# A three-layer network in float32 on one core: head and expert stages rebuilt, with a new order of VectorE's work at the first experts

## The chip, the cores and the metric

The kernel runs on one core of a Trainium2 chip. The metric is the device time of one execution in microseconds (us). It is given as the median of several runs; beside it stands one profiled execution, from which every row of the trace below comes. The engines are TensorE (PE; its weight loads are PEld), VectorE (DVE), ScalarE (ACT), GpSimd (POOL) and SyncE (SP), which issues all the DMAs.

## The reference, cut to what matters

The input is x of 4 sequences x 512 tokens x 128 features, 2048 tokens in all. Four residual layers follow one another:

```python
x = x + ssm(layernorm(x))          # state-space layer with 64 complex states, a scan over the 512 tokens
x = x + experts(layernorm(x))      # 8 experts, each token weighted by its best 2
x = x + attention(layernorm(x))    # 16 heads of 64, a relative-position bias, softmax over 512 keys
x = x + experts(layernorm(x))      # the same experts and weights again

def experts(xt):                   # router_w 8x128, w_gate/w_up 8x128x256, w_down 8x256x128
    top, idx = top_k(xt @ router_w.T, 2)
    g = sigmoid(top); g = g / (g.sum(-1) + 1e-10)
    for e in range(8):
        ge = sum(where(idx == e, g, 0))
        out += ge[:, None] * ((silu(xt @ w_gate[e]) * (xt @ w_up[e])) @ w_down[e])
```

Every expert is computed for every token and multiplied by its gate, which is zero for most tokens.

## The kernel before

The 2048 tokens are four chunks of 512. A large matrix product is made of three passes over numbers that are split into a rounded high part and a remainder (`hi`, `lo`, type fp32r): hi x hi, hi x lo, lo x hi (`three`, lines 222 to 224). The high part is a ScalarE cast, the low part a subtraction, on VectorE for activations (`ln_low`) and on GpSimd for the experts' hidden values (`hid_lo`, line 688) and weights (`w_lo`, line 674). The order of work on each engine is written out by hand, and semaphores join the engines.

The program has these stages.

1. **Head.** The parameters of the state-space layer, the rotation angles (VectorE), the first layer norm (VectorE, with `ln_norm` at line 263), four rounds of state products, scan and output (`ssm_in`, `states`, `ssm_out`, `residual`), and the preparation of the attention's weights between them.
2. **Experts, k = 0.** Routing first: router products, a copy, four small transposes, the best two of eight, the gates, and a transpose of the gates that goes to DRAM and comes back spread over all partitions (`gate_all`). It is done for chunks 0 to 2 together and then for chunk 3. Then 32 steps, one for each expert and chunk: step `s` is `gate_up` for half 0 (6 matmuls), `down` for the step two before it (6), `gate_up` for half 1 (6). For each half ScalarE makes the silu, VectorE the product (`hid<-silu,bank`, line 550) and the multiplication by the gate (line 559), ScalarE the high part (line 476) and GpSimd the low part (line 688). The steps run expert after expert, in iterations `i` of two experts (8 steps, parities 0 and 1); the middle iterations are a loop on the engine.
3. **Weights of the next expert.** While an expert's four steps run, the other parity's weights are split in three pieces (gate, up, down columns). At steps 0, 1 and 2 of the expert, ScalarE rounds a piece after that step's `high` (line 494), and GpSimd subtracts it between its two `hid_lo` of the step (line 674). TensorE waits for the third piece before the next expert's first `gate_up`.
4. **Attention.** 128 slots of two heads and 128 queries each. A slot has scores, transposes for two slots back, the product with the values for six slots back, and in some slots a job in the one free bank (a projection, values, an output part).
5. **Experts, k = 1**, as k = 0, with all loads and the routing after the attention; then the output is stored.

Of the kernel before, what the change touches and what calls it, by code (L numbers as in the profile page):

```python
# [14 lines left out]
BANK = 512  # L20
MAGIC = 1.5 * 2.0**23
GRID = 1.5 * 2.0**10

TWO_PI_1 = 6.28125
TWO_PI_2 = float(np.float32(round((2 * math.pi - TWO_PI_1) * 2**20) / 2**20))
TWO_PI_3 = float(2 * math.pi - TWO_PI_1 - TWO_PI_2)
PI_BELOW = 3.1415925
# [6 lines left out]
def build(nc, t, out):  # L34
# [14 lines left out]
    O_SLOTS = 6  # L49
    assert D == P and 2 * N == P and 2 * DK == P and S == BANK and MT == 2 and CH == B  # L50

    with ExitStack() as ctx:
# [3 lines left out]
        def sb_in(stack, name, shape, dt=F32):  # L56
            return stack.enter_context(nc.sbuf_tensor(name, shape, dt))

        def sb(name, shape, dt=F32):
            return sb_in(ctx, name, shape, dt)  # L60
# [14 lines left out]
        half_var = sb("ln_half_var", [P, TILES])  # L75
        rstd = sb("ln_rstd", [P, TILES])
        newt = sb("ln_newton", [P, TILES])
        rwh = sb("router_hi", [P, E], F32R)
        rwl = sb("router_lo", [P, E], F32R)
        band = sb("bias_band", [P, H, BAND])  # L80
        ah = sb("qk_hi", [P, H, P], F32R)
        al = sb("qk_lo", [P, H, P], F32R)
        wvh = sb("wv_hi", [P, H * DK], F32R)
        wvl = sb("wv_lo", [P, H * DK], F32R)
        wo = sb("wo_sb", [P, PAIRS, D])


        with ExitStack() as st:
            w_raw = sb_in(st, "w_raw", [P, 2, EW])
            w_hi = sb_in(st, "w_hi", [P, 2, EW], F32R)  # L90
            w_lo = sb_in(st, "w_lo", [P, 2, EW], F32R)
            logits = sb_in(st, "logits", [P, TILES, E])
            top = sb_in(st, "top", [P, TILES, E])
            topi = sb_in(st, "topi", [P, TILES, E], U32)
            topf = sb_in(st, "topf", [P, TILES, 2])
            gw = sb_in(st, "gate_w", [P, TILES, 2])
            gsum = sb_in(st, "gate_sum", [P, TILES, 1])
            pick = sb_in(st, "pick", [P, 2, TILES, E])
            gates = sb_in(st, "gates", [P, TILES, E])
            gatesT = sb_in(st, "gatesT", [QT * E, CH, P])  # L100
            logitsT = sb_in(st, "logitsT", [E, 3, BANK])

            gate_all = sb_in(st, "gate_all", [P, 2, TILES * P])
            y_sum = sb_in(st, "y_sum", [P, CH, BANK])
            silu = sb_in(st, "silu", [P, MT, BANK])
            hid = sb_in(st, "hid", [P, 2, MT, BANK])
            hid_hi = sb_in(st, "hid_hi", [P, 2, MT, BANK], F32R)
            hid_lo = sb_in(st, "hid_lo", [P, 2, MT, BANK], F32R)
        FRONT = 6 * EW + (4 * TILES * E + 4 * TILES + TILES + 2 * TILES * E) + CH * P + 3 * BANK


        with ExitStack() as st:
            sb_in(st, "experts_front", [P, FRONT])
            oh = sb_in(st, "onehot", [NB, 2 * BANK])
            table = sb_in(st, "table_sb", [NB, H])
            bias_row = sb_in(st, "bias_row", [H, 2 * BANK])
            wqT = sb_in(st, "wqT", [P, PAIRS, P])
            wkT = sb_in(st, "wkT", [P, PAIRS, P])
            wv = sb_in(st, "wv_sb", [P, H * DK])
            af = sb_in(st, "qk_f32", [P, H, P])  # L120
            par = sb_in(st, "ssm_par", [P, t["ssm_par"].shape[1]])
            bT = sb_in(st, "bT", [P, 2, P])
            bTh = sb_in(st, "bT_hi", [P, 2, P], F32R)
            bTl = sb_in(st, "bT_lo", [P, 2, P], F32R)
            wcT = sb_in(st, "wcT", [P, 2, P])
            mcs = sb_in(st, "state_out", [P, 2, D])
            wd = sb_in(st, "wd_f32", [P, D])
            wdh = sb_in(st, "wd_hi", [P, D], F32R)
            wdl = sb_in(st, "wd_lo", [P, D], F32R)
            lam = sb_in(st, "lam", [P, 4])  # L130
            cols = sb_in(st, "cols", [P, 16])
# [13 lines left out]
        with ExitStack() as st:  # L145

            qkh = sb_in(st, "qkT_hi", [P, 2, 2, S], F32R)
            qkl = sb_in(st, "qkT_lo", [P, 2, 2, S], F32R)
            prob = sb_in(st, "prob", [P, PROBS, 2, S])
            probT = sb_in(st, "probT", [P, 2, 2, QT, S])  # L150
            oT = sb_in(st, "oT", [P, O_SLOTS, S])
            v = sb_in(st, "v", [P, QT, H * DK])
            peak = sb_in(st, "peak", [P, PROBS, 2])
            total = sb_in(st, "total", [P, PROBS, 2])
            inv = sb_in(st, "inv_total", [P, PROBS, 2])
# [10 lines left out]
        ld_attn = sem("ld_attn")  # L166
        ld_band = sem("ld_band")
        bias_out = sem("bias_out")
        s_cw = sem("s_cw")
        s_tp = sem("s_tp")  # L170
        s_ev = sem("s_ev")
        s_ah = sem("s_ah")
# [16 lines left out]
        def ln_sems(k):  # L189
            return {n: sem(f"ln{k}_{n}") for n in ("dve", "xn", "t", "hi", "lo")}  # L190
# [267 lines left out]
        def moe_scalar(act, k):  # L458
# [51 lines left out]
            if k == 0:  # L510
                first_buffers_free(act)
# [890 lines left out]
```

## Time and profile before

| | |
|---|---|
| median of 3 runs | 902.26 us (902.04 to 903.08) |
| profiled execution | 905.03 us, span of its trace 903.2 us |
| mean granted TensorE clock | 0.968 |
| busy share | PE 91%, DVE 73%, ACT 57%, POOL 49% |

The span is what the trace covers, from its first instruction to its last; the time of the execution holds about 2 us more, before and after it. Busy time is what an engine spent on instructions in the trace, and it tells of a bound only inside a stage, since the stages have different limits. A few per cent of the matmul records are missing, so counts of matmuls in a window come out low.

### The profile page before, as it was taken

How to read it: one execution, taken by the hardware profiler on the slowest of the kernel's cores; microseconds unless marked ns; L12 is line 12 of the kernel's file. 1: busy time of each engine (PE TensorE's matmuls, PEld its weight loads, DVE VectorE, ACT ScalarE, POOL GpSimd, SP SyncE). 2: the span in 40 equal slices, each digit the busy share in tenths (PEclk: the TensorE clock that was granted, in tenths of full speed). 3: DMA queues.
4: the chain of work that ended last, by engine and by line, in shares of the span. 5: the costliest groups of instructions: out<-in, count | busy, mean ns of one | idle time of the engine just before them, and what ended most of it. 6: DMA issues, size and time to landing. Idle time of an engine off the chain costs nothing.

```text
span 903.2 us, 13948 instructions
## 1 busy us (share of the span) xinstructions
PE 819.9 (91%) x4320; PEld 547.8 (61%) x4320; DVE 658.6 (73%) x1664; ACT 515.1 (57%) x1121; POOL 442.9 (49%) x464
## 2 busy tenths in 40 slices
PE   1867699999779999999999999999999996899997
PEld 0555478888545556556556565565565564688875
DVE  7998477787788776767776767767777646687876
ACT  2214365665466766666566665657656644556664
POOL 3350389998234333433333333334333423789994
PEclk9698899999999999999999999999999997999999
DMA  7001345438300000000000000000000012436621
GB/s 210 3 1 30 85 74 85 90 84 241 122 1 1 1 1 1 1 1 1 1 1 1 1 2 1 1 1 1 1 1 1 1 37 72 96 80 84 79 70 47
DMA packets 53265, 36.40 MB, mean 40 GB/s; under 512 B 2209, under 2 KB 50721, under 8 KB 53201
## 3 DMA queue, kind: packets, MB, share of 16 engines
q1 hardware_dynamic: 53200, 35.61, 17.7%
q8 instruction: 33, 0.54, 0.3%
q14 instruction: 32, 0.25, 0.1%
HBM read 34.35 MB, written 1.25 MB: 39 GB/s over the span
## 4 chain that ended last, share of the span: by engine, by line
PE 75%; DVE 11%; issue 4%; POOL 3%; DMA 3%; ACT 2%; SPq 0%; POOLq 0%; DVEq 0%; ACTq 0%
PE bank L839 13%; PE bank L822 12%; PE bank L809 11%; PE bank L222 10%; PE bank L411 9%; PE bank L224 8%; PE bank L223 8%; PE bank L775 3%; POOL hid_lo L688 3%; DMA gates<-gatesT 1%; DVE x_norm L263 1%; DMA gate_all<-gates 1%; DVE ln_stats L237 1%; DVE prob L884 1%; PE bank L277 1%
## 5 line engine op out<-in xcount | busy, mean ns | idle before, releaser
L1028 POOL TENSOR_SCALAR prob<-prob,inv_total 128x512 f32<-128x512 f32 x256 | 175.1, 697 | 317.3 <-DVE inv_total L873 317.3
L688 POOL TENSOR_TENSOR hid_lo<-hid,hid_hi 128x512 fp32r<-128x512 f32 x128 | 192.1, 1518 | 92.3 <-ACT hid_hi L476 90.4
L977 ACT ACTIVATE prob<-prob,peak 128x512 f32<-128x512 f32 x256 | 185.8, 726 | 47.5 <-DVE peak L884 47.5
L884 DVE CUSTOM_DVE_ANT_0 prob<-bank,bias_band 128x512 f32<-128x512 f32 x256 | 166.6, 689 | 31.0 <-PE bank L809 25.1
L822 PE MATMUL bank<-ident,prob 128*128 128x128 f32 x1024 | 136.5, 277 | 3.1 <-ACT probT L983 1.8
L839 PE MATMUL bank<-probT,v 128*64 128x512 f32 x512 | 138.2, 620 | 0.8 <-ACT oT L988 0.8
L559 DVE TENSOR_TENSOR hid<-hid,gate_all 128x512 f32<-128x512 f32 x128 | 123.6, 970 | 19.0 <-DMA gate_all<-gates 15.2
L822 PEld LDWEIGHTS bank<-ident,prob 128*128 128x128 f32 x1024 | 119.8, 143 | 23.9 <-issue 7.2
L550 DVE TENSOR_TENSOR hid<-silu,bank 128x512 f32<-128x512 f32 x128 | 87.0, 684 | 57.8 <-PE bank L224 39.7
L476 ACT CAST hid_hi<-hid 128x512 fp32r<-128x512 f32 x128 | 78.8, 618 | 61.2 <-DVE hid L559 58.1
L466 ACT ACTIVATE silu<-bank 128x512 f32<-128x512 f32 x128 | 76.1, 599 | 61.8 <-PE bank L224 57.5
L222 PE MATMUL bank<-xT_hi,w_hi 128*128 128x512 f32 x256 | 103.8, 405 | 8.1 <-DVE hid L550 8.1
L891 DVE COPY probT<-bank 128x512 f32<-128x512 f32 x128 | 87.6, 685 | 21.6 <-PE bank L822 21.6
L224 PE MATMUL bank<-xT_hi,w_lo 128*128 128x512 f32 x256 | 102.7, 401 | 0.0
L223 PE MATMUL bank<-xT_lo,w_hi 128*128 128x512 f32 x256 | 102.5, 400 | 0.0
L809 PEld LDWEIGHTS bank<-qkT_hi 64*128 64x128 f32 x256 | 23.8, 183 | 100.5 <-issue 92.3
L972 ACT CAST qkT_hi<-bank 128x512 fp32r<-128x512 f32 x64 | 37.6, 588 | 79.4 <-PE bank L224 79.3
L983 ACT COPY probT<-bank 128x512 f32<-128x512 f32 x128 | 73.4, 573 | 14.4 <-PE bank L822 14.4
L873 DVE RECIPROCAL inv_total<-total 128x2 f32<-128x2 f32 x128 | 21.2, 166 | 64.8 <-ACT prob L977 63.6
L809 PE MATMUL bank<-qkT_hi 64*128 64x512 f32 x256 | 63.9, 495 | 0.0
L222 PEld LDWEIGHTS bank<-xT_hi,w_hi 128*128 128x128 f32 x256 | 49.2, 192 | 23.3 <-DVE hid L550 6.3
L224 PEld LDWEIGHTS bank<-xT_hi,w_lo 128*128 128x128 f32 x256 | 49.0, 192 | 11.3
(171 smaller groups left out, 1266.1 us busy)
## 6 DMA issues: line engine op xcount, KB each, us to landing
gate_all<-gates SPq DMA_DIRECT2D x12, 1024.0 KB, 15.5
bias_band<-bias_rows SPq DMA_DIRECT2D x16, 448.0 KB, 11.5
gate_all<-gates SPq DMA_DIRECT2D x16, 256.0 KB, 4.9
w_raw<-in_w_gate SPq DMA_DIRECT2D x16, 128.0 KB, 14.5
w_raw<-in_w_up SPq DMA_DIRECT2D x16, 128.0 KB, 10.5
w_raw<-in_w_down SPq DMA_DIRECT2D x16, 128.0 KB, 8.7
x_res<-in_x SPq DMA_DIRECT2D x4, 256.0 KB, 4.7
out<-x_res SPq DMA_DIRECT2D x4, 256.0 KB, 2.3
```

Of the source, the lines that this page charges most:

```text
L222: nc.tensor.matmul(dst, lh, rh, start=start, stop=False)
L223: nc.tensor.matmul(dst, lh, rl, start=False, stop=False)
L224: return nc.tensor.matmul(dst, ll, rh, start=False, stop=stop)
L559: nc.vector.tensor_tensor(hid[:, buf, m, :], hid[:, buf, m, :], gate_all[:, par, c * BANK:(c + 1) * BANK], ALU.mult).then_inc(q["gm"], 1)
L688: nc.gpsimd.tensor_tensor(hid_lo[:, buf, m, :], hid[:, buf, m, :], hid_hi[:, buf, m, :].bitcast(F32), ALU.subtract).then_inc(q["hl"], 1)
L809: last = nc.tensor.matmul(bank[2 * (n % 2) + h][:, :], ql[rows, u % 2, 0, q], kl[rows, u % 2, 1, :], start=(i == 0), stop=(i == 2))
L822: last = nc.tensor.transpose(bank[4 + h][:, j * P:(j + 1) * P], prob[:, n % PROBS, h, j * P:(j + 1) * P], ident[:, :])
L839: last = nc.tensor.matmul(bank[PV_BANK][h * DK:(h + 1) * DK, :], v[:, kt, col], probT[:, u % 2, h, kt, :], start=(kt == 0), stop=(kt == QT ...
L884: nc.vector.tensor_tensor_reduce(out=prob[:, buf, h, :], in0=bank[2 * (n % 2) + h][:, :], in1=row_bias, scale=-1.0, scalar=NEG_START, op0= ...
L891: nc.vector.tensor_copy(probT[:, u % 2, 1, :, qt * P:(qt + 1) * P], bank[5][:, :].rearrange("p (k q) -> p k q", k=QT)).then_inc(a_eb, 1)
L977: nc.scalar.activation(prob[:, buf, h, :], prob[:, buf, h, :], ACT.Exp, bias=peak[:, buf, h:h + 1], scale=-1.0, accum_out=total[:, buf, h: ...
L1028: nc.gpsimd.tensor_scalar(prob[:, buf, h, :], prob[:, buf, h, :], inv[:, buf, h:h + 1], 1.0, ALU.mult, ALU.mult).then_inc(a_n, 1)
```

## The change

- **Head.** The state layer's input and output products use plain float32 operands (`bT`, `wd`, `xf`), one matmul in the place of three, and the hi/lo splits of these operands go. The rotation angles are made before the first layer norm. The normalisation moves from VectorE to ScalarE (`ln_apply`, Identity with scale and bias), and so do the copies of `wcT` and `state_out`. GpSimd's order is: bias for four chunks, then `turn_back` with the low parts of weights between.
- **Routing.** Router products have the tokens as the stationary operand (8 small matmuls a chunk), which makes the transposes of logits unnecessary. The gates of expert 0 are spread over the partitions by TensorE into PSUM (`route_spread`) for all chunks at k = 0 and for chunk 3 at k = 1. Routing is done in halves at k = 0, and for chunks 0 to 2 inside the attention's last sequence at k = 1.
- **First experts.** Products (VectorE's first multiplication) run ahead of the gates through four `hid` buffers. VectorE's order at k = 0 is the first two chunks' routing, then the run-ahead products, then the low parts of chunks 2 and 3.
- **Order of experts.** The first and last iterations go by chunk, alternating the two experts; the middle ones go by expert. The weights' pieces move: ScalarE and GpSimd now do them as `FIRST_PIECES`, `MIDDLE_PIECES` and `LAST_PIECES` say (position of the step in the iteration: parity, iterations ahead, piece). TensorE waits for the gate and up pieces (`wu`) apart from the down piece (`wd`).
- **Stage borders.** The last sums of the experts are folded into their last steps and into the attention's entry; the weights, routing and first products of k = 1 start inside the attention's last sequence and its last products (`leave`).
- The loops are written out. Buffers are placed by hand in one map, and each gate load is now one chunk (256 KB).

```diff
+        BY_CHUNK = [(0, 0), (0, 1), (1, 0), (1, 1), (0, 2), (0, 3), (1, 2), (1, 3)]
+        BY_EXPERT = [(0, 0), (0, 1), (0, 2), (0, 3), (1, 0), (1, 1), (1, 2), (1, 3)]
+        FIRST_PIECES = {6: [(0, 1, 0)], 7: [(0, 1, 1)]}
+        MIDDLE_PIECES = {0: [(0, 0, 2)], 1: [(1, 0, 0)], 2: [(1, 0, 1)], 3: [(1, 0, 2)], 6: [(0, 1, 0)],
+                         7: [(0, 1, 1)]}
+        LAST_PIECES = {0: [(0, 0, 2), (1, 0, 0)], 1: [(1, 0, 1)], 2: [(1, 0, 2)]}
...
+        def gate_up(pe, k, i, order, pos, half, first=False):
...
+            if half == 0 and first_of(order, pos):
+                pe.wait_ge(q["wu"], 2 * i + par_ + 1)
...
+        def scalar_step(act, k, i, pos, pieces, deep=2, deep_before=2):
+            s = 8 * i + pos
+            silu_of(act, k, s, 0)
+            high_of(act, k, s - 1, (pos - 1) % 8, 1, deep_before if pos == 0 else deep)
+            silu_of(act, k, s, 1)
+            high_of(act, k, s, pos, 0, deep)
+            for par_, ahead, piece in pieces.get(pos, ()):
+                weight_high(act, k, i, par_, ahead, piece)
...
+        def pool_step(pool, k, i, pos, pieces, deep=2, first=False):
+            s = 8 * i + pos
+            low_of(pool, k, s, pos, 0, deep, first and pos < 2)
+            for par_, ahead, piece in pieces.get(pos, ()):
+                weight_low(pool, k, 2 * (i + ahead) + par_, par_, piece)
+            low_of(pool, k, s, pos, 1, deep, first and pos < 2)
...
+            def leave():
+                step = lambda pos: expert_step(pe, 1, 0, ENDS, pos, True)
+                part = lambda pos, half: gate_up(pe, 1, 0, BY_CHUNK, pos, half, True)
+                transposes(SLOTS - 2)
+                pv(SLOTS - PV_LAG)
+                pe.wait_ge(a_m, 2 * SLOTS - 2)
+                part(0, 0)
...
+                part(3, 1)
+                route_logits(pe, 1, 3, JOB_BANK)
+                step(4)
+                route_turn(pe, 1, 1)
+                route_spread(pe, 1, 3)
+                step(5)
...
+            for c in (0, 1):
+                route_sum(dve, 0, c, 4 + c)
+            route_max(dve, 0, 0)
+            route_index(dve, 0, 0, 0, 2)
+            early(0)
+            route_weights(dve, 0, 0)
+            route_pick(dve, 0, 0)
+            early(1)
+            late(0)
+            ln_low(dve, 1, 2, 6)
+            ln_low(dve, 1, 3, 7)
+            early(2)
+            late(1)
+            early(3)
```

## Rows read from the trace of the kernel before

**Rows 1.** Stretches: from:to, length, busy PE, PEld, DVE, ACT, POOL, clock, DMA, GB/s.
```profile
0.00:74.31 74.31, 41.61 (x210) 31.04 (x210) 62.74 (x185) 17.54 (x30) 27.40 (x32) 0.86 0.23 65
74.31:120.86 46.55, 31.26 (x113) 22.53 (x112) 28.95 (x123) 20.47 (x39) 16.70 (x14) 0.85 0.26 66
120.86:229.98 109.12, 109.12 (x469) 87.66 (x467) 86.57 (x104) 65.92 (x123) 98.56 (x69) 1.00 0.56 130
229.98:244.87 14.89, 10.49 (x50) 7.54 (x50) 12.22 (x36) 5.46 (x10) 3.25 (x3) 1.00 0.17 67
244.87:720.48 475.61, 463.02 (x2749) 273.22 (x2749) 342.84 (x973) 310.93 (x747) 172.37 (x252) 0.99 0.00 1
720.48:782.95 62.47, 49.81 (x240) 34.52 (x239) 33.76 (x135) 25.87 (x50) 23.39 (x24) 0.89 0.24 63
782.95:892.10 109.15, 109.15 (x469) 87.44 (x467) 86.46 (x104) 65.80 (x123) 97.89 (x69) 1.00 0.45 71
892.10:903.20 11.10, 5.45 (x28) 3.83 (x28) 5.09 (x6) 3.10 (x6) 3.36 (x3) 1.00 0.32 94
```

**Rows 2.** TensorE's timeline, first matmul of steps 10, 11 and 12: start, us, instruction.
```profile
799.65 0.39 PE L222 MATMUL bank<-xT_hi,w_hi 128*128 128x512 f32 x1
...
803.81 0.39 PE L222 MATMUL bank<-xT_hi,w_hi 128*128 128x512 f32 x1
...
808.03 0.49 PE L222 MATMUL bank<-xT_hi,w_hi 128*128 128x512 f32 x1
```

**Rows 3.** GpSimd's timeline in step 11, and in step 18 for step 17.
```profile
803.68 3.07 POOL L688 TENSOR_TENSOR hid_lo<-hid,hid_hi 128x512 fp32r<-128x512 f32 x2
806.70 1.19 POOL L674 TENSOR_TENSOR w_lo<-w_raw,w_hi 128x256 fp32r<-128x256 f32 x1
...
835.47 1.20 POOL L674 TENSOR_TENSOR w_lo<-w_raw,w_hi 128x256 fp32r<-128x256 f32 x1
```

**Rows 4.** ScalarE's timeline, step 10's high part and weight piece.
```profile
803.82 0.61 ACT L476 CAST hid_hi<-hid 128x512 fp32r<-128x512 f32 x1
804.33 0.41 ACT L494 CAST w_hi<-w_raw 128x256 fp32r<-128x256 f32 x1
```

**Rows 5.** VectorE's timeline, a gate multiplication while GpSimd subtracts.
```profile
888.83 1.66 DVE L559 TENSOR_TENSOR hid<-hid,gate_all 128x512 f32<-128x512 f32 x1
```

**Rows 6.** Stretches in and behind a wait of TensorE, columns as in Rows 1.
```profile
112.20:114.75 2.55, 0.01 (x1) 0.00 (x0) 1.93 (x4) 1.89 (x4) 1.19 (x1) 1.00 0.07 21
116.60:119.30 2.70, 2.67 (x6) 2.17 (x7) 2.19 (x3) 0.90 (x2) 2.70 (x2) 0.50 0.51 88
```

**Rows 7.** VectorE's timeline in the head.
```profile
7.09 1.65 DVE L237 BATCH_NORM_STATS2 ln_stats<-x_res 128x6 f32<-128x128 f32 x8 [1.13 <-DMA x_res<-in_x]
...
13.10 3.09 DVE L263 TENSOR_SCALAR x_norm<-x_res,ln_mean_var,ln_rstd 128x128 f32<-128x128 f32 x8
...
16.11 0.48 DVE L1278 TENSOR_SCALAR bias_band<-bias_band,cols 128x512 f32<-128x512 f32 x1
...
21.53 1.28 DVE L288 TENSOR_TENSOR xT_lo<-bank,xT_hi 128x512 fp32r<-128x512 f32 x2
...
33.97 0.69 DVE L1311 TENSOR_TENSOR bias_band<-bank,bias_band 128x512 f32<-128x512 f32 x1
...
56.16 2.42 DVE L237 BATCH_NORM_STATS2 ln_stats<-x_res 128x6 f32<-128x128 f32 x12
```

**Rows 8.** TensorE's timeline in the head, two plain float32 matmuls of 512 columns.
```profile
33.40 3.59 PE L1116 MATMUL bank<-onehot,table_sb 32*16 32x512 f32 x4
```

**Rows 9.** VectorE's timeline, first and last row of the last chunk's routing, k = 1.
```profile
761.14 0.19 DVE L353 COPY logits<-bank 128x32 f32<-128x32 f32 x1 [0.30 <-PE bank L309]
...
764.58 0.19 DVE L380 TENSOR_TENSOR gates<-pick 128x32 f32<-128x32 f32 x1
```

**Rows 10.** SyncE's and VectorE's timelines, chunk 3's gates through DRAM, k = 0.
```profile
103.70 0.34 SPq L643 DMA_DIRECT2D gates<-gatesT  x1
...
112.14 1.29 DVE L559 TENSOR_TENSOR hid<-hid,gate_all 128x512 f32<-128x512 f32 x2 [3.89 <-DMA gate_all<-gates]
```

More of the change, by code:

```diff
@@ L88, in build @@
[L88 to L108, printed above, removed]
@@ new lines, in down @@
+        def down(pe, k, i, orders, pos, first=False):
+            q, m = MOE[k], MEM[k]
+            now, before = orders
+            at = pos - LAG
+            order, i_at = (now, i) if at >= 0 else (before, i - 1)
+            s, at = 8 * i + at, at % 8
+            par_, c = order[at]
+            pe.wait_ge(q["hl"], 2 * s + 2)
+            if first_of(order, at):
+                pe.wait_ge(q["wd"], 2 * i_at + par_ + 1)
+            fresh = first and pos >= LAG and par_ == 0
+            for h in range(MT):
+                col = slice(2 * FH + h * D, 2 * FH + (h + 1) * D)
+                wh, wl = m["w_hi"][:, par_, col], m["w_lo"][:, par_, col]
+                hh, hl = m["hid_hi"][:, at % 2, h, :], m["hid_lo"][:, at % 2, h, :]
+                for n, (w, r) in enumerate(((wh, hh), (wh, hl), (wl, hh))):
+                    last = nc.tensor.matmul(bank[4 + c][:, :], w, r, start=(fresh and h == n == 0),
+                                            stop=(h == MT - 1 and n == 2), skip_group_check=True)
+            last.then_inc(q["d"], 1)
@@ new lines, in expert_step, with sums_turn @@
+        def expert_step(pe, k, i, orders, pos, first=False):
+            gate_up(pe, k, i, orders[0], pos, 0, first)
+            down(pe, k, i, orders, pos, first)
+            gate_up(pe, k, i, orders[0], pos, 1, first)
+        def sums_turn(pe, k, c):
+            pe.wait_ge(MOE[k]["y"], c + 1)
+            for n in range(QT):
+                last = nc.tensor.transpose(bank[4 + c][:, n * P:(n + 1) * P], MEM[k]["y_sum"][:, c, n * P:(n + 1) * P],
+                                           ident[:, :])
+            last.then_inc(MOE[k]["yt"], 1)
@@ new lines, in product, with products @@
+        def product(dve, k, s, pos, half, deep=2, first=False):
+            q, m = MOE[k], MEM[k]
+            dve.wait_ge(q["sg"], 2 * s + half + 1)
+            dve.wait_ge(q["u"], 2 * s + half + 1)
+            if not first:
+                dve.wait_ge(q["hl"], 2 * s + half + 1 - 2 * deep)
+            nc.vector.tensor_tensor(m["hid"][:, pos % deep, half, :], m["silu"][:, half, :], bank[2 * half + 1][:, :],
+                                    ALU.mult).then_inc(q["mul"], 1)
+        def products(dve, k, s, pos, deep=2, first=False):
+            for half in range(MT):
+                product(dve, k, s, pos, half, deep, first)
@@ new lines, in enter, with steady @@
+            def enter(high_0, high_1):
+                ln_apply(act, 2, 0, 0)
+                high_0()
+                ln_high(act, 2, 0, 4)
+                high_1()
+                for what in "qk":
+                    high(what, 0, EARLY_BANK[what])
+                for kt in (1, 3):
+                    value(0, 0, kt, EARLY_BANK[kt])
+            def steady():
+                for n in range(SLOTS):
+                    if n >= PV_LAG + QT and (n - PV_LAG) % QT == 0:
+                        pair_out((n - PV_LAG) // QT - 1)
```

1375 lines of the change are left out of this document (781 added, 594 removed).

## The prediction, made before the changed kernel was run

> **What bounds the kernel now.** I cut the span by stage first and asked in each stretch whether TensorE is busy throughout [rows 1]. In the experts' steady part it is: 109.12 us of 109.12 for steps 6 to 31 at k = 0, and 109.15 of 109.15 at k = 1. That is 26 steps of 4.20 us, 18 matmuls each, 0.233 us a matmul. In the attention it is nearly so, 463.0 of 475.6 us for 127 slots. The rest is where time can be won. The head up to the first `gate_up` takes 74.3 us, in which VectorE is busy for 62.7. Routing and the first steps take 46.6 us with TensorE busy for 31.3. The passage into the attention takes 14.9, and the one from the last slot's scores to step 6 of k = 1 takes 62.5 with TensorE busy for 49.8, at a mean clock of 0.89. The tail behind the last `gate_up` is 11.1. Together 209 us are not steady. Next I read the timelines of the steady steps for slack, since the change moves work there too. GpSimd is busy for 98.6 of 109.1 us, and that is what decides this forecast.
>
> **The weight pieces.** This is the term with the largest sum, and it costs. In step 10 ScalarE rounds the third piece of the next expert at 804.33 [rows 4], 4.7 us after the step's first matmul at 799.65 [rows 2], since it stands behind that step's `high`. GpSimd subtracts it at 806.70, behind two `hid_lo`, and ends at 807.89 [rows 3]: 8.2 us after the step began. Step 12, which waits for it, begins at 808.03 [rows 2]. So the kernel before has exactly two steps (8.4 us) of lead and uses all of it. Another instance, in step 17, which began at 782.95 + 11 x 4.20 = 829.15, ends at 836.67 [rows 3], 7.5 us after. A piece that is handled in a step is thus ready 7.5 to 8.2 us after the step's start.
>
> In the new tables the last piece that `wu` needs for the next iteration's first expert is handled at position 7, and position 0 follows 4.2 us later. TensorE is in order, so it waits, and the `down` and second half behind it wait too. The wait is 3.3 to 4.0 us, less up to 0.4 because VectorE stops and no longer contends with GpSimd: 2.9 to 4.0, I take 3.3. It comes at each of the three borders between iterations. Inside a middle iteration the up piece is handled at position 2 and needed at 4, the old lead of two steps, so nothing is lost there. In the last iteration the second expert is needed at position 2 already, while its up piece is handled at position 1, and position 0 has two pieces for GpSimd: again one step of lead, plus up to one more subtraction (1.2 us). I take 3.6, between 3.3 and 5. The down pieces have `wd` and a later use, so they cost nothing; their cover is the two steps of lag of `down`.
>
> TensorE's clock falls behind such a wait. After the 2.55 us without a matmul at 112.2 the granted clock is 0.50 (the 1.2 GHz level) from 116.6 to 119.3, where six matmuls take 2.7 instead of 1.4 us [rows 6]. A wait here is longer, but isolated. I take 0.9 a wait, between 0 and 1.3. The Trainium skill ("TensorE: Matmul & The Clock Gate", section "HAM oscillation") says that a pause which recurs in each turn of a loop sends the array back to its slow clock each time; by that rule each wait would cost the full 1.3 and the sum below would be 2.4 us more. The one wait shown agrees.
>
> Per expert stage the borders 1-2 and 2-3 and the last iteration's wait give 2 x 3.3 + 3.6 = 10.2, the clock 3 x 0.9 = 2.7, and two `sums_turn` (4 transposes each, 0.45) now before the last `gate_up` 0.9: **+13.8**, twice **+27.6**. The border 0-1 stands in the next two terms.
>
> **Head to step 8 of k = 0.** Before, step 8 begins at 120.86 + 2 x 4.20 = 129.3 [rows 1].
> - VectorE did layer norm from 7.09, its normalisation from 13.10 to 16.11, then the rotation to 21.53, and began the first state product at 33.97 [rows 7]. Now the rotation (5.4) comes first, about 6 to 11.5, then the norm without normalisation (6.0, or 5 with less GpSimd work beside it) to about 16.5. ScalarE normalises in 1, TensorE turns, ScalarE copies, and two plain float32 matmuls follow at 1.8 each on the slow clock [rows 8]. The first state product is possible at 22, 12 us earlier.
> - The four rounds took 22.2 us (33.97 to 56.16) [rows 7]. GpSimd now adds the bias of all four chunks before its first `turn_back`, and chunk 3 is normalised at about 29. Its low parts of weights stand between the others. I let this cost 2: the last output comes 10 us earlier.
> - From the second layer norm to the first `gate_up` it took 18.2 (56.16 to 74.31). Two chunks at a time and ScalarE's normalisation give about 13, so the first `gate_up` starts at 60, 14 us earlier.
> - From there to step 8 took 55.0. TensorE's own work is 132 matmuls, 31 us. I walked the written order: `late(1)` sits until `route_spread(0, 1)`, which TensorE does after step 3 and four router groups; chunk 3's gates for expert 1 still go through DRAM, 8.4 us from 103.70 to 112.14 [rows 10], and hold position 6 and 7; then the border wait of about 3. It comes to 51, with one fall of the clock. Step 8 at 111: **-18.3**. If GpSimd's order costs nothing and the waits overlap, it is -26; if VectorE's chain is as slow as before from the first `gate_up` on, -10.
>
> **Entry of the attention.** Before 14.9. VectorE now has one chunk's norm (about 4.4 us) between steps 5, 6 and 7, where it has 22.5 us of idle in 109 [rows 1], about 0.9 a step. So 3 us of it push the last product. Sums 2 and 3, their turns and `down(31)` now stand before the first scores. I get 16.2 from the last `gate_up` to the scores: **+1.3** (-2 to +4).
>
> **Attention.** Three chunks' router products are 8 matmuls each with a weight load apiece. No row shows the form; at 0.12 each 3 us in all, no less than 1 and at 0.233 no more than 5.6. VectorE's routing (3.6 us for one chunk alone [rows 9], some 5.5 for three) goes into slots in which VectorE is idle for a quarter of the time (343 of 476 us busy): I take 1. **+4.0** (1 to 8). Weight loads and their splits there are free; GpSimd is idle for 64% of that stage.
>
> **Last scores to step 8 of k = 1.** Before 62.5 + 8.4 = 70.9. TensorE's 49.8 us hold about 5 lost to the slow clock, about 5 of old routing and one step; 37 are left up to step 5. The layer norm of chunk 3 waits for the last output projection and holds `route_logits(3)` by 2.5. Then VectorE must finish step 4, route chunk 3 (3.6 plus the hand-overs of ScalarE), while TensorE stands for about 7: step 5 at 47, step 8 at 47 + 12.6 + the border's 3 + 3 of slow clock, 65.7: **-5.2** (-11 to +1).
>
> The tail is the same chain (product, gate, high, low, `down`, sum, turn, add, store): 0.
>
> **Sum.** -18.3 + 1.3 + 4.0 - 5.2 + 27.6 = **+9.4**. On the span of 903.2 that is 912.6; the median of the runs is 0.9 below that span, so 912.
>
> In steps where `hid` is multiplied by `gate_all`, VectorE needs 1.66 us while GpSimd runs [rows 5]; with the gates of the first steps in PSUM that may become short. The Trainium skill ("SBUF — State Buffer", section "Who interferes with whom") says that a VectorE operation with two SBUF inputs contends with GpSimd's reads and one with a single SBUF input doesn't. By it three first steps would gain 1 us each on VectorE, of which my walk already holds most; the row agrees as far as it goes.
>
> **Rivals.**
> 1. The border waits don't come, because ScalarE and GpSimd reach positions 6 and 7 early enough. For it speaks only that GpSimd has two positions (4 and 5) without a piece to catch up; against it, that the lead is set by the step's own `high`, not by backlog (7.5 us in step 17, after such a pause). It would give 912 - 12.9 x 2 = 886, with the 0-1 waits 884. It decides the sign when a wait with its clock costs less than 2.7 us instead of 4.3. Chance 0.15.
> 2. Head and second entry gain their upper ends (-26, -11), with the waits as reckoned: 898. Chance 0.13.
> 3. Gate and weight loads also come late (now 256 KB each, behind first gates on SyncE's queue), and every wait brings the clock down: 12 us more, 924. Chance 0.10.
> 4. The terms cancel within 0.2% (about what a measurement of this kernel can tell from no change). Chance 0.05.
>
> My forecast, 905 to 920, has 0.57. Its range is from the waits' bounds (2.9 to 4.0) and half of the head's. Taking in rivals 2 and 3 and the edge of rival 1 gives 887 to 924. Faster: rivals 1 and 2 and 0.01: 0.29. Same 0.05. Slower 0.66.
>
> **What would show it.** In the profile after: TensorE idle for 3 to 4 us before `gate_up` at steps 8, 16, 24 and at step 26 of both expert stages, ended by `w_lo`; the stretch from step 8 to the last `gate_up` 114 us instead of 100.8; a first `gate_up` at about 60 and step 8 at about 111. It is wrong if TensorE runs through these borders, if the head gains over 25 us, or if the routing inside the attention stops TensorE for more than 8.

## The result and the profile after

The changed kernel is slower: 932.69 us (929.83 to 934.32, 4 runs) against 902.67 us (902.04 to 904.29, 4 runs) of the kernel before beside it, ratio 1.0326 with a 95% interval of 1.0292 to 1.0361. The forecast was 912, with a range up to 924. The direction was right, and the size was too small by some 20 us (30.0 measured, 9.7 forecast). The profiled execution has a span of 928.0 us; its time, 929.83, was the shortest of the four, so the spans differ by 24.8 us and the medians by 30.0.

The stretches of the changed kernel, cut at the same events as the prediction's sum, with the columns of [rows 1]:

```profile
0.00:62.10 62.10, 36.11 (x168) 26.16 (x169) 49.99 (x153) 27.97 (x61) 27.11 (x28) 0.87 0.26 78
62.10:115.30 53.20, 40.56 (x184) 31.25 (x184) 34.42 (x120) 28.31 (x52) 20.89 (x17) 0.92 0.25 52
115.30:235.27 119.97, 109.24 (x440) 86.66 (x440) 81.18 (x105) 60.48 (x113) 88.64 (x63) 0.93 0.43 121
235.27:251.88 16.61, 11.45 (x44) 8.67 (x43) 8.60 (x20) 6.68 (x13) 2.90 (x2) 0.79 0.00 0
251.88:728.85 476.97, 464.39 (x2774) 273.60 (x2773) 347.56 (x1016) 312.69 (x754) 176.55 (x258) 0.99 0.02 4
728.85:797.78 68.93, 53.28 (x258) 39.01 (x256) 41.43 (x89) 29.05 (x52) 26.12 (x21) 0.92 0.21 47
797.78:917.18 119.40, 109.09 (x440) 86.84 (x440) 79.37 (x95) 60.54 (x114) 89.10 (x63) 0.93 0.25 59
917.18:928.00 10.82, 4.61 (x21) 2.94 (x20) 4.22 (x5) 2.17 (x4) 2.55 (x2) 0.95 0.25 73
```

The borders are the first `gate_up`, step 8 of k = 0, the end of the last `gate_up`, the scores of slots 0 and 127, step 8 of k = 1, and the end of the last `gate_up` again. Against [rows 1] they give this account, in us:

| term | predicted | measured | from |
|---|---|---|---|
| head to step 8, k = 0 | -18.3 | -14.0 | 115.3 against 129.3 |
| step 8 to last `gate_up`, k = 0 | +13.8 | +19.2 | 119.97 against 100.7 |
| entry of the attention | +1.3 | +1.7 | 16.61 against 14.89 |
| attention | +4.0 | +1.4 | 476.97 against 475.61 |
| last scores to step 8, k = 1 | -5.2 | -2.0 | 68.93 against 70.9 |
| step 8 to last `gate_up`, k = 1 | +13.8 | +18.6 | 119.40 against 100.8 |
| tail | 0 | -0.3 | 10.82 against 11.10 |
| sum | +9.4 | +24.6 | span +24.8 |

TensorE's timeline has these waits for a weight piece (start, duration, instruction, in brackets the idle time ahead of it and what ended it):

```profile
115.30 0.80 PE L243 MATMUL bank<-xT_hi,w_hi 128*128 128x512 f32 x1 [6.26 <-POOL w_lo L710]
...
155.01 0.50 PE L243 MATMUL bank<-xT_hi,w_hi 128*128 128x512 f32 x1 [3.36 <-POOL w_lo L710]
...
193.55 0.79 PE L243 MATMUL bank<-xT_hi,w_hi 128*128 128x512 f32 x1 [3.36 <-POOL w_lo L710]
...
207.04 0.80 PE L243 MATMUL bank<-xT_hi,w_hi 128*128 128x512 f32 x1 [3.59 <-POOL w_lo L710]
...
797.78 0.79 PE L243 MATMUL bank<-xT_hi,w_hi 128*128 128x512 f32 x1 [3.25 <-POOL w_lo L710]
...
837.61 0.50 PE L243 MATMUL bank<-xT_hi,w_hi 128*128 128x512 f32 x1 [3.36 <-POOL w_lo L710]
...
876.16 0.80 PE L243 MATMUL bank<-xT_hi,w_hi 128*128 128x512 f32 x1 [3.36 <-POOL w_lo L710]
...
889.67 0.80 PE L243 MATMUL bank<-xT_hi,w_hi 128*128 128x512 f32 x1 [3.59 <-POOL w_lo L710]
```

They stand at steps 8, 16, 24 and 26 of both stages, the eight places that the prediction named. Seven of them last 3.25 to 3.59 us, against 3.3 and 3.6 predicted; the first one of k = 0 lasts 6.26. GpSimd's timeline shows how such a wait ends:

```profile
150.76 3.51 POOL L720 TENSOR_TENSOR hid_lo<-hid,hid_hi 128x512 fp32r<-128x512 f32 x2
154.24 0.72 POOL L710 TENSOR_TENSOR w_lo<-w_raw,w_hi 128x256 fp32r<-128x256 f32 x1
```

ScalarE rounds the up piece at 151.98, in step 15; GpSimd takes it behind the `hid_lo` before it and ends at 154.96, and step 16 begins at 155.01.

Behind each wait TensorE's clock is at or near its slow level. The stretches of 4 us behind the first two:

```profile
115.30:119.30 4.00, 4.00 (x9) 3.14 (x10) 0.88 (x2) 1.10 (x2) 1.14 (x1) 0.50 0.61 161
155.01:159.01 4.00, 4.00 (x11) 3.12 (x12) 1.25 (x2) 1.10 (x2) 1.28 (x1) 0.57 0.60 48
```

A granted clock of 0.50 is the 1.2 GHz level: 9 matmuls are recorded in 4 us, where 17 are at full clock (experiment 4). From the restart on, the clock stays at 0.50 for 6.0 us behind step 8 of k = 0, for 6.2 behind step 8 of k = 1, and until 2.9 to 3.9 us behind the restart at the other six: ```profile
115.30:121.30 6.00, 6.00 (x14) 4.74 (x15) 1.57 (x2) 1.10 (x2) 1.28 (x1) 0.50 0.52 140
193.55:196.40 2.85, 2.85 (x7) 2.27 (x8) 0.00 (x0) 1.10 (x2) 0.00 (x0) 0.50 0.26 84
797.78:804.00 6.22, 6.22 (x15) 4.87 (x16) 1.57 (x2) 1.10 (x2) 1.28 (x1) 0.50 0.46 115
```

At 0.50 half of such time is lost: 3.0 and 3.1 us behind the two steps 8, and 1.4 to 1.7 behind each of the other six, 15.5 in all, 1.9 on average. Over the whole stretch from step 8 to the last `gate_up` TensorE is busy for 109.24 us at a mean clock of 0.93; in the kernel before it was 100.7 at 1.00. Of these 8.5 us the two turns of sums are 0.9; the other 7.6 are about twice the 0.9 a wait that I had given to the clock.

## The experiments

Theory A is the prediction's mechanism with measured sizes: a piece that is handled one step before its use is late, and each wait costs its length and a slow clock behind it. Two further names are used. B: GpSimd is overloaded, so that a piece that is moved only moves the wait. C: something else in the changed kernel holds the pieces up.

**1. The middle iterations' pieces two positions earlier.** The wait on `u` in `weight_high` follows the new position.

```diff
-        MIDDLE_PIECES = {0: [(0, 0, 2)], 1: [(1, 0, 0)], 2: [(1, 0, 1)], 3: [(1, 0, 2)], 6: [(0, 1, 0)],
-                         7: [(0, 1, 1)]}
+        MIDDLE_PIECES = {0: [(0, 0, 2)], 1: [(1, 0, 0)], 2: [(1, 0, 1)], 3: [(1, 0, 2)], 4: [(0, 1, 0)],
+                         5: [(0, 1, 1)]}
```

> The changed kernel with only this moved: in the two middle iterations the gate and up pieces of the next iteration's first expert are handled at positions 4 and 5 in place of 6 and 7, so that they have three steps of lead at the borders 1-2 and 2-3. Theory A (too little lead): the waits of 3.36 us at steps 16 and 24 of both stages go, with the slow clock behind them. TensorE is busy 8.4 us longer from step 8 to the last gate_up than 24 steps of 4.20, less 0.9 for two turns of sums: 7.5, or 1.9 a wait. So 4 x (3.4 + 1.9) = 21 us less, 911 to 912; with the 0.9 of the prediction for the clock it would be 17 less, 916. Theory B (GpSimd and ScalarE are behind altogether, a piece moved is a wait moved): waits come back at positions 4 to 7 and the time stays above 922.

Measured: 907.58 us (7 runs), 1.0047 of the kernel before (1.0026 to 1.0067): 25.1 less than the changed kernel. The waits at steps 16 and 24 are gone, four in all. What is left of them in the table of waits (total, number, longest):

```profile
PE bank L243 <- POOL w_lo L710: 16.4, 4, 5.6
```

B falls: nothing comes back between positions 4 and 7. That is 6.3 us for each wait removed by the medians and 5.6 by the profiled spans (928.0 and 905.5), against 5.3 expected.

**2. All pieces early.** The middle iterations are as in 1. At the other borders ScalarE and GpSimd take the gate and up pieces at the beginning of a step, ahead of its other work (position 6 of the first iteration, position 0 of the last); SyncE issues the loads of iteration 1 before the second half's gates.

```diff
+        FIRST_FRONT = {6: [(0, 1, 0), (0, 1, 1)]}
+        LAST_FRONT = {0: [(1, 0, 0), (1, 0, 1)]}
...
             s = 8 * i + pos
+            for par_, ahead, piece in front.get(pos, ()):
+                weight_high(act, k, i, par_, ahead, piece)
...
+            first_gates(sp, 0, 0)
+            load_weights(sp, 0, 2, 1, 0)
+            first_gates(sp, 0, 1)
```

> As e1_middle_early, and the other two borders as well: in the first iteration both pieces are handled at the very beginning of position 6, ahead of that step's silu and low parts; in the last iteration the second expert's two pieces at the beginning of position 0; the down piece of the next first expert at position 6 of a middle iteration; SyncE issues the weights of iteration 1 before the second half's gates. Theory A: all eight waits (6.26, 3.25, 4 x 3.36, 2 x 3.59) go or fall below 1 us, with 1.9 of slow clock each: 30.1 + 15 = 45 us less, 888, and 893 at most if half a microsecond stays at each of four borders. Theory B: two pieces in one step put GpSimd behind by 2.4 us, down waits for hid_lo, above 905.

Measured: 888.22 us, 0.9833 (0.9799 to 0.9868), as A had it. No wait for `w_lo` is left, and the two stretches from step 8 on are:

```profile
113.46:215.30 101.84, 101.39 (x441) 81.44 (x439) 79.86 (x108) 61.56 (x115) 93.82 (x65) 1.00 0.48 147
772.00:874.00 102.00, 102.00 (x445) 82.43 (x444) 78.38 (x98) 62.20 (x116) 93.61 (x66) 1.00 0.33 72
```

TensorE has 0.45 us of idle in the first and none in the second (which is cut at round numbers), at a clock of 1.00. The rest of the rebuild is thus worth 16 us against the kernel before (904.18 us in these runs), once the eight waits are out. Busy time in the first stretch is 101.39, against 109.24 in the changed kernel with the same work: 7.85 us for the slow clock behind four waits, 2.0 on average.

**3. Work for TensorE during the waits.** The pieces stay where the change put them.

```diff
+            if half == 0 and (pos == 0 and i > 0 or pos == 2 and i == HALF - 1):
+                pe.wait_ge(q["mul"], 2 * s - 1)
+                for _ in range(12):
+                    nc.tensor.matmul(bank[0][:, :], xh[:, 0:P], xh[:, 0:BANK], start=True, stop=True)
```

> The changed kernel, with 12 more matmuls of 512 columns (2.8 us at full clock, into a bank that is free and overwritten right after) on TensorE just ahead of each of the eight waits for w_lo. The pieces come no earlier, so the end of each wait stays; only TensorE has work during it. Theory A1 (the 7.5 us a stage beyond waits and turns are the slow clock behind the waits): granted clock from step 8 to the last gate_up rises from 0.93 to 0.98 or more, and 13 to 15 us go: 918 to 920. With 0.9 a wait, as in the prediction, 926. Theory A2 (they are something else): 932 or more.

Measured: 917.22 us, 1.0158 (1.0123 to 1.0194): 15.5 less. From step 8 to the last `gate_up`:

```profile
115.28:228.55 113.27, 110.64 (x476) 88.17 (x476) 83.60 (x105) 60.54 (x113) 88.84 (x63) 1.00 0.45 127
```

The clock is 1.00 throughout, and the stretch is 113.27 long in place of 119.97, although 36 more matmuls lie inside it. In the same places a wait now ends with 0.64 to 1.80 us left. So the part beyond the waits is the clock: 15.5 / 8 = 1.9 us a wait by the medians, and 13.8 / 8 = 1.7 by the profiled spans (928.0 and 914.2).

**4. The kernel before, with late pieces alone.** ScalarE's first four steps are written out, and get the one call that the shift needs there (`expert_high(0, 3, ...)`); without it that piece is never rounded and the program stands still, so the first version had no time.

```diff
-                par, piece = j // CH, j % CH
-                if piece == 3 or (last and par == 1):
+                par, piece = j // CH, j % CH - 1
+                if piece < 0 or (last and par == 1):
...
             high(3, 1, 0, False)
+            expert_high(0, 3, True, False)
...
-                        if m == 1 and c < 3 and not (last and par == 1):
-                            split(2 * i + par + 1, 1 - par, c, first and par == 0)
+                        if m == 1 and c > 0 and not (last and par == 1):
+                            split(2 * i + par + 1, 1 - par, c - 1, first and par == 0)
```

> The kernel before with one part alone of the change: the three pieces of the next expert's weights are handled at steps 1, 2 and 3 of an expert in place of 0, 1 and 2, by ScalarE and GpSimd (k = 0 and 1). Theory A: one step of lead is left at all 14 borders between experts. TensorE waits 3.4 us at each and loses 1.9 to the clock, sizes from the runs so far: 14 x 5.3 = 74 us more, 978; with the clock term of the prediction 14 x 4.2 = 59 more, 963. Theory C (what makes the changed kernel wait is something of the changed kernel, its order by chunk, its gates or loads, and not the lead): below 915.

Measured: 973.29 us against 906.63, 1.0742 (1.0695 to 1.0788), 66.7 more. C falls: the old kernel makes the same waits from this part alone, at all 14 borders. The first three and four of the later ones:

```profile
116.68 0.79 PE L222 MATMUL bank<-xT_hi,w_hi 128*128 128x512 f32 x1 [9.85 <-POOL w_lo L675]
...
138.84 0.79 PE L222 MATMUL bank<-xT_hi,w_hi 128*128 128x512 f32 x1 [3.44 <-POOL w_lo L675]
...
161.77 0.79 PE L222 MATMUL bank<-xT_hi,w_hi 128*128 128x512 f32 x1 [3.41 <-POOL w_lo L675]
...
856.17 0.49 PE L222 MATMUL bank<-xT_hi,w_hi 128*128 128x512 f32 x1 [3.43 <-POOL w_lo L675]
...
876.50 0.49 PE L222 MATMUL bank<-xT_hi,w_hi 128*128 128x512 f32 x1 [3.34 <-POOL w_lo L675]
...
896.89 0.49 PE L222 MATMUL bank<-xT_hi,w_hi 128*128 128x512 f32 x1 [3.40 <-POOL w_lo L675]
...
917.11 0.79 PE L222 MATMUL bank<-xT_hi,w_hi 128*128 128x512 f32 x1 [3.26 <-POOL w_lo L675]
```

Twelve waits are 3.24 to 3.44 us long and the first of each stage 9.85 and 8.85 (there the third piece stands behind chunk 3's gates); together 58.8. The clock was expected to take 14 x 1.9 = 27 us more. It took 18.9, and the granted clock tells why:

```profile
138.84:142.84 4.00, 4.00 (x9) 3.17 (x10) 0.83 (x2) 1.10 (x2) 1.06 (x1) 0.50 0.33 68
856.17:860.17 4.00, 4.00 (x17) 3.29 (x18) 2.11 (x2) 1.32 (x3) 1.30 (x1) 1.00 0.31 75
876.50:880.50 4.00, 4.00 (x17) 3.29 (x18) 2.11 (x2) 1.32 (x3) 1.30 (x1) 1.00 0.37 78
896.89:900.89 4.00, 4.00 (x17) 3.30 (x18) 2.13 (x2) 1.34 (x3) 1.29 (x1) 1.00 0.66 61
```

Behind the wait at 138.84 it is 0.50; behind three consecutive waits of 3.34 to 3.43 us in the second stage it is 1.00, and so it is behind those at 183.50 and 248.26. Five of the 14 cost no clock. The other nine cost 1.4 to 2.8 us each. In the same place as each stage's first wait the kernel before had two shorter waits (1.61 and 2.54 us at k = 0, 1.62 and 2.09 at k = 1) and one slow stretch that cost 1.7, so the account closes: 58.8 + 18.9 - 7.9 - 3.4 = 66.4, and the spans differ by 66.3.

**5. The order of k = 1's first steps.** On top of 2, `step(5)` goes ahead of chunk 3's gates on TensorE, and its silus ahead of their copy on ScalarE.

```diff
                 step(4)
+                step(5)
                 route_turn(pe, 1, 1)
                 route_spread(pe, 1, 3)
-                step(5)
```

> e2_all_early (888.2 us) with step 5 of k = 1 moved ahead of the turn and the spread of chunk 3's gates on TensorE, and its two silus ahead of the copy of the gates on ScalarE. TensorE waits 5.95 us there for the routing in e2_all_early. Theory A: one step of 4.2 us fits into that wait, and since step 6 needs only the product of step 5, which VectorE makes right behind the routing while TensorE turns and spreads, 4 us go: 884. Theory B: VectorE is the bound here and not the order, the wait reappears before step 6: 887 or more.

Measured: 884.31 us (877.62 to 886.89), 0.974 (0.9687 to 0.9792). The wait for the gates went from 5.95 to 2.85 us. 3 us of the expected 4 are in the trace. The median is 3.9 below that of 2, and the two intervals don't overlap, so the step's place matters; how much it is worth is less sure, since the kernel before measured 2.4 us more beside 5 than beside 2, and the profiled spans differ by 1.9 (885.7 and 883.8).

**6. SyncE's order alone**, in the changed kernel (the last three lines of 2's diff).

> The changed kernel with SyncE's order alone changed: the weights of iteration 1's first expert are loaded ahead of the second half's gates, at k = 0 and k = 1. At the border 0-1 of k = 0 TensorE waits 6.26 us in the changed kernel and 3.4 at the others, and ScalarE's first weight piece there waits 1.83 us for the load. Theory A (the load is what is late beyond the lead): the wait falls from 6.26 to 4.0 to 4.5, all others stay at 3.2 to 3.6, 930 to 931 in time. Theory B (VectorE is late there, with the gates): 6.0 or more stays.

Measured: 929.96 us, 1.0267 (1.0234 to 1.03). The first border of k = 0:

```profile
116.85 0.80 PE L243 MATMUL bank<-xT_hi,w_hi 128*128 128x512 f32 x1 [4.11 <-POOL w_lo L711]
```

4.11 in place of 6.26, so 2.15 us of that wait were the load, as A had it. The changed kernel's ScalarE shows the same from its side:

```profile
108.83 0.41 ACT L557 CAST w_hi<-w_raw 128x256 fp32r<-128x256 f32 x1 [1.83 <-DMA w_raw<-in_w_down]
```

In 6 this wait of ScalarE is gone. The other 0.7 above 3.4 us is not told apart. The profiled execution as a whole is no shorter (928.0 us both), and step 8 begins later, at 116.85, because the clock fell twice more in the head, first behind a wait of 1.91 us for a product. In the changed kernel the same wait lasted 1.89 us and the clock stayed up. First 6, then the changed kernel, from the restart on:

```profile
71.25:76.75 5.50, 5.50 (x14) 4.24 (x15) 3.32 (x14) 3.10 (x5) 0.00 (x0) 0.50 0.01 3
```

```profile
71.07:76.57 5.50, 5.50 (x25) 4.17 (x26) 5.19 (x18) 3.98 (x6) 0.00 (x0) 1.00 0.01 3
```

**7 and 8. Two other orders on VectorE at k = 0**, on top of 5: the first products ahead of the routing (7), and the low parts of chunks 2 and 3 ahead of the gates (8).

```diff
             early(0)
+            early(1)
+            ln_low(dve, 1, 2, 6)
+            ln_low(dve, 1, 3, 7)
             route_weights(dve, 0, 0)
             route_pick(dve, 0, 0)
-            early(1)
             late(0)
-            ln_low(dve, 1, 2, 6)
-            ln_low(dve, 1, 3, 7)
             early(2)
```

> e5_leave with another order on VectorE at the first experts of k = 0: the products of step 0 ahead of the first tokens' routing, those of step 1 inside it, then the gates. TensorE waits 1.7 us for the product of step 0 in e2_all_early, and that goes; the gates come up to 2.5 us later, and the spread of expert 0's gates stands in TensorE's way. If this order matters: 1 to 2 us less or up to 2 more than e5_leave. If the next thing waited for is the same for every order: within 0.5 us in the trace at step 8, and no difference in time.

> e5_leave with a third order on VectorE at the first experts of k = 0: routing up to the indices, the products of steps 0 and 1, then the low parts of chunks 2 and 3, and only then the weights and the gates of the first two chunks. The gates come 2.5 us later than in e5_leave, and TensorE has the spread of expert 0's gates ahead of steps 2 and 3: it stands for 2 to 3 us, and the clock may fall: 2 to 5 us more than e5_leave. If VectorE's order here has slack: no difference.

Measured: 887.89 us for 7 (0.9793, 0.9763 to 0.9823) and 885.93 for 8 (0.9771, 0.9743 to 0.9798), against 884.31 with the change's order. The intervals overlap. 7 was expected from 2 us below 5 to 2 above and came 3.6 above; 8, expected 2 to 5 above, came 1.6 above in time. The traces tell them apart: the wait for the product goes in 7, and both have TensorE wait for the gates instead.

```profile
75.48 1.12 PE L384 MATMUL bank<-ident,gates 128*128 128x128 f32 x4 [5.07 <-DVE gates L463]
```

```profile
80.84 1.12 PE L384 MATMUL bank<-ident,gates 128*128 128x128 f32 x4 [4.52 <-DVE gates L463]
```

From the first turn of the norm (57.84 us in 5, 56.22 in 7, 59.94 in 8) to the first half of position 7 it takes 49.9 us in 5, 52.3 in 7 and 54.8 in 8. The nine profiled kernels with the change's order need 45.6 to 49.9 us there (5 is the slowest of them), so 7 and 8 are above all of them, by 2.3 and 4.9 us at least; that is one profile each, and the times alone don't tell them apart.

**9. Idle matmuls in two other waits**, on top of 5.

> e5_leave (884.3 us) with idle matmuls in two waits outside the borders: 10 of 512 columns (2.3 us) ahead of the turn of chunk 0's norm at the entry of the attention, where TensorE waits 3.33 us and then runs at half clock for 4.8 us; 8 of them (1.9 us) ahead of chunk 3's router products at k = 1, where it waits 3.0. If the clock falls behind a wait of 3 us wherever it is: 2.4 us less at the entry and 1 to 2 at k = 1, about 881. If there it falls for another reason: 884, and the granted clock behind the entry stays at 0.5.

Measured: 883.16 us, 0.9759 (0.9729 to 0.9788): no difference to 5.

```profile
214.89 3.39 PE L914 MATMUL bank<-xT_hi 128*128 128x512 f32 x10 [2.29 <-DVE hid L602]
...
740.31 1.97 PE L965 MATMUL bank<-xT_hi 128*128 128x512 f32 x8
743.51 0.28 PE L364 MATMUL bank<-router_hi_lo,xT_hi 128*128 128x16 f32 x1 [1.22 <-DVE xT_lo L324]
```

The first set had to wait for a product itself, 2.29 of the 3.33 us, then ran partly at the slow clock (10 matmuls took 3.39 us) and put off the turn by 2 us, which ate what the earlier return of the clock gave. The second left 1.22 of 3.0 us open, and the clock still fell, from 745.4 to 748.8. The expectation was wrong in that the bank comes free late. What a full cover would give at these places stays open.

**10 and 11. Two small operations that wait for GpSimd.** In 10, run once, they have two SBUF inputs; in 11 they stand ahead of step 30. Both on top of 5.

```diff
                 ln_moments(dve, 2, 0, 1)
+                ln_scale(dve, 2, 0, 1)
+                ln_shift(dve, 2, 0, 1)
             vector_step(dve, k, i, BY_CHUNK, 6)
-            if k == 0:
-                ln_scale(dve, 2, 0, 1)
-                ln_shift(dve, 2, 0, 1)
```

> e5_leave with the first two operations of ln_scale, 128 x 4 elements each, as an addition of two SBUF inputs and an operation of two SBUF inputs in place of two with one input and a constant. Ahead of the attention they take 1.26 and 1.22 us each while GpSimd subtracts, and 0.16 elsewhere. If the form with one SBUF input is what waits for GpSimd: they fall to 0.16 and the wait of 3.33 us for x_norm to about 1.3. The Trainium skill (SBUF — State Buffer, section on who interferes with whom) says that an operation with two SBUF inputs waits for GpSimd too: by it both stay at about 1.2.

> e5_leave with chunk 0's ln_scale and ln_shift for the attention ahead of step 30 on VectorE, where GpSimd is idle for 2.1 us, in place of behind it. The two small operations then take 0.16 each and x_norm comes 1.5 us or more earlier: the wait at the entry falls from 3.33 to about 1.7, while step 31 waits for the product of step 30 about 1.9 us more than the 0.4 now. Theory A (order only shifts the wait): no difference, 884 within 2. Theory B: the clock then stays up and 2 to 3 us go.

The two operations and GpSimd's subtraction about that time, in 10 and then in 11:

```profile
208.92 1.25 DVE L270 TENSOR_TENSOR ln_var<-ln_mean_var,ln_consts 128x4 f32<-128x4 f32 x1
210.21 1.22 DVE L272 SCALAR_TENSOR_TENSOR ln_rstd<-ln_var,ln_consts 128x4 uint32<-128x4 uint32 x1
...
208.41 3.00 POOL L729 TENSOR_TENSOR hid_lo<-hid,hid_hi 128x512 fp32r<-128x512 f32 x2 [2.15 <-ACT hid_hi L549]
```

```profile
205.58 0.17 DVE L269 TENSOR_SCALAR ln_var<-ln_mean_var 128x4 f32<-128x4 f32 x1
205.78 0.17 DVE L270 TENSOR_SCALAR ln_rstd<-ln_var 128x4 uint32<-128x4 uint32 x1
...
204.36 1.30 POOL L725 TENSOR_TENSOR hid_lo<-hid,hid_hi 128x512 fp32r<-128x512 f32 x1 [1.28 <-ACT hid_hi L546]
```

For these two operations the form changes nothing, the place does: 1.25 and 1.22 us beside a subtraction of GpSimd, 0.17 each where GpSimd is idle (its subtraction ends at 205.66, 0.08 us behind the start of the first one). In 11 the entry's wait fell from 3.33 to 1.52 us and that of step 31 for the product of step 30 rose from 0.45 to 2.73. The time is 882.75 us (0.9744, 0.9684 to 0.9804), within 2 us of 5: the wait was shifted, as A had it. 10 gave 882.16 in its single run.

### The profile page after: what moved, and what is told of

Its sections match the earlier page's. It is cut to its first block and busy times, and to the rows that moved or that the text cites. A ratio compares the mean times of both kernels' runs of the same rounds, so it can differ in the third digit from the quotient of the medians.

```text
span 928.0 us, 13407 instructions
## 1 busy us (share of the span) xinstructions
PE 828.7 (89%) x4320; PEld 555.1 (60%) x4320; DVE 646.8 (70%) x1600; ACT 527.9 (57%) x1161; POOL 433.9 (47%) x454
## 3 DMA queue, kind: packets, MB, share of 16 engines
HBM read 33.04 MB, written 1.25 MB: 37 GB/s over the span
## 5 line engine op out<-in xcount | busy, mean ns | idle before, releaser
L720 POOL TENSOR_TENSOR hid_lo<-hid,hid_hi 128x512 fp32r<-128x512 f32 x128 | 191.1, 1508 | 146.1 <-ACT hid_hi L543 144.1
L243 PE MATMUL bank<-xT_hi,w_hi 128*128 128x512 f32 x256 | 109.6, 428 | 35.9 <-POOL w_lo L710 30.1
L624 DVE TENSOR_TENSOR hid<-hid,gate_all 128x512 f32<-128x512 f32 x118 | 119.8, 1017 | 8.9 <-DMA gate_all<-gates 1.1
L245 PE MATMUL bank<-xT_hi,w_lo 128*128 128x512 f32 x256 | 106.4, 416 | 0.0
L244 PE MATMUL bank<-xT_lo,w_hi 128*128 128x512 f32 x256 | 106.3, 415 | 0.0
L543 ACT CAST hid_hi<-hid 128x512 fp32r<-128x512 f32 x128 | 78.5, 616 | 47.6 <-DVE hid L624 41.4
L243 PEld LDWEIGHTS bank<-xT_hi,w_hi 128*128 128x128 f32 x256 | 51.3, 200 | 55.0 <-POOL w_lo L710 33.6
L245 PEld LDWEIGHTS bank<-xT_hi,w_lo 128*128 128x128 f32 x256 | 51.4, 201 | 12.5
```

What stands on the lines that cost most here:

```text
L243: nc.tensor.matmul(dst, lh, rh, start=start, stop=False)
L244: nc.tensor.matmul(dst, lh, rl, start=False, stop=False)
L245: return nc.tensor.matmul(dst, ll, rh, start=False, stop=stop)
L624: nc.vector.tensor_tensor(buf, buf, gate, ALU.mult).then_inc(q["gm"], 1)
L720: nc.gpsimd.tensor_tensor(m["hid_lo"][:, pos % 2, half, :], m["hid"][:, pos % deep, half, :], m["hid_hi"][:, pos % 2, half, :].bitcast(F32 ...
```

## Why the forecast was right in direction and too small

**The weight pieces: right in place and length, wrong in what follows.** "One step of lead" is what decides. Moving two pieces by two positions removes exactly the waits at 16 and 24 (1), moving all removes all (2), and the kernel before gets them by that part alone (4). The length was given as 3.3 and 3.6 and measured as 3.25 to 3.59.

**The clock is the step that failed.** The prediction says "I take 0.9 a wait, between 0 and 1.3". Measured are 1.9 to 2.0 on average, 15.5 us in all, and each of the eight was above the 1.3: 1.4 to 1.7 behind six waits, 3.0 and 3.1 behind the two steps 8. The 1.3 came from [rows 6], where I counted six slow matmuls in 2.7 us. That was a cut out of a longer stretch: the clock is at its slow level from 116.1 to 119.5, 3.4 us, which costs 1.6. The trace of the kernel before also held what I needed, a slow stretch that begins 1 us behind the restart from a wait of 3.26 us (ended at 750.00), with TensorE busy throughout:

```profile
116.10:119.50 3.40, 3.29 (x9) 2.32 (x8) 2.69 (x3) 1.40 (x3) 3.40 (x4) 0.51 0.51 87
...
750.00:751.00 1.00, 0.99 (x6) 0.78 (x7) 1.00 (x2) 0.30 (x1) 0.00 (x0) 1.00 0.25 73
751.00:754.40 3.40, 3.40 (x10) 2.62 (x9) 1.98 (x4) 1.82 (x4) 1.90 (x2) 0.50 0.21 53
```

That is 1.7 us for one fall, where I took 0.9 and bounded it by 1.3; six of the eight falls are of that size or a little less. The 3 us behind the steps 8 have no such row. Their waits are 6.26 and 3.25 us long, so the length doesn't explain them, and why the clock stayed down for so long there is open. Six of the waits lie in the two stretches from step 8 on; the falls behind the steps 8 lie there too, and I had put them ahead: the cost of a fall belongs behind the step that waited. With the four falls as measured, 3.02 + 1.71 + 1.44 + 1.52 = 7.7, the first stretch is 100.7 + 10.3 of waits + 7.7 + 0.9 = 119.6, against 119.97 in the trace.

The Trainium skill ("TensorE: Matmul & The Clock Gate", section "HAM oscillation") has each recurring pause send the array back to its slow clock. In the changed kernel all eight do, and the rule was nearer than my choice. The fourth experiment limits it: pauses of the same length in the same loop, one each 20 to 23 us, left the clock at 1.00 five times in 14.

**Head to step 8 (-18.3, measured -14.0).** The first `gate_up` began at 62.1 us against 60 predicted, and the border wait at step 8 was 6.26 us, against the prediction's "about 3" and 3.4 at the other borders (the walk's 51 us became 53.2). Rival 3 had this mechanism: the load comes late behind the first gates on SyncE's queue. It holds at one border of eight, for 2.15 us (6). Without this excess of 2.9 the head would be at -16.9.

**Last scores to step 8 of k = 1 (-5.2, measured -2.0).** Three waits there total 12 us (2.99 for the norm, 3.02 for the low parts, 5.95 for the gates). The prediction had two of them, 2.5 and 7. Not told apart is how the remaining 3 us divide between the second wait and slow clock.

**Entry, attention and tail** were right within 0.4, 2.6 and 0.3 us. The router products inside the attention cost 0.11 us each (seven start between 679.29 and 679.96), just below the 0.12 to 0.233 that I had.

**The gates in PSUM** were expected to make VectorE's multiplication short beside GpSimd, by [rows 5]. They do: four of them take 2.47 us, 0.62 each, inside a run of GpSimd's subtractions, where the kernel before needed 1.66 for one.

```profile
97.53 2.47 DVE L624 TENSOR_TENSOR hid<-hid,bank 128x512 f32<-128x512 f32 x4
...
96.92 7.66 POOL L720 TENSOR_TENSOR hid_lo<-hid,hid_hi 128x512 fp32r<-128x512 f32 x6 [3.92 <-ACT hid_hi L543]
```

It was already in the walk of the head, and no separate gain came of it: TensorE waited for the first gates, the routing and the weights there, not for these.

**The range.** Its upper end of 924 came from rival 3, which needed late loads as well as a clock that falls each time. The clock at its measured size adds 15.5 - 8 x 0.9 = 8.3 to +9.4; the longer first border adds 2.9 and the later first `gate_up` 2.1; what is left, 4.4, is mostly in the last scores to step 8 of k = 1 and is not told apart; entry, attention and tail give 2.5 back: +24.6. The bound for the clock had been set by one instance, and it carried eight occurrences: it should have had the widest interval in the sum. A further 5 us lie between spans and medians: the profiled execution of the kernel before was 2.4 us above its median and that of the changed kernel 2.9 below.

**The rivals.** That the waits do not come (886) is refuted, since all eight came. Its price was nearly right: a kernel with this head and without them runs at 888. The upper ends of head and entry (898) are refuted too: the head gave 14 us and not 26. Rival 3 had the falls of the clock right and the late loads wrong but for one border, and its 12 us were too few as well.

## What to carry to other kernels

A schedule that hands over one step before the use needs its producer's own latency, counted from the start of the step and through every engine of the chain. If that is more than one step, each hand-over stalls, and spare capacity of the producer doesn't help: in 1 and 2 GpSimd did the same subtractions and the waits were gone. Price a stall of TensorE as its length plus a slow stretch behind it (here from nothing to 3.1 us), read that stretch from where the clock falls to where it is back, and give it the widest bound, for it multiplies. When a large rebuild comes out slower, look for one small table in it: here two entries moved by two positions gave back 25 us, and all pieces moved, with one load, turned +3.3% into -1.7%, and with one step reordered into -2.6%.

## What the runs showed of the hardware that was not expected

- Within one kernel and one loop, TensorE's granted clock fell behind waits of 3.24 to 3.44 us seven times and stayed at 1.00 behind waits of 3.26 to 3.43 us five times, so their length does not tell the cases apart. It fell behind a wait of 1.91 us in 6 and stayed up behind the same wait of 1.89 us in the changed kernel. The start of a fall also moved between executions, and the head with it: in kernels whose head was the same the clock fell between 54.1 and 58.6 us and the norm's turn ahead of the first `gate_up` started between 56.2 and 60.1 us, in the same order.
- A VectorE operation on 128 x 4 elements took 1.2 us while GpSimd subtracted 128 x 512 elements, and 0.17 when it was idle (11). The 1.2 us are the same with one SBUF input and a constant (5 and the changed kernel) as with two SBUF inputs (10). In 10 the second one ends at 211.43 and GpSimd's second subtraction at 211.41: it looks like a wait for the end of the other instruction and no share of bandwidth. The page "SBUF — State Buffer" of the Trainium skill (section "Who interferes with whom") says that the shared pair of ports is an exclusive lock, and names two SBUF inputs and the faster modes of an operation with a constant as what needs it; 10 and the changed kernel agree with it.
